# Cross attention in a decoder layer: one exponential over two PSUM banks in place of two, and its place before the copy of the weighed values

## The reference, cut to what matters

```python
q, k, v = query @ Wq, ctx @ Wk, ctx @ Wv          # 32, 8 and 8 heads of 16
q, k = rope(q), rope(k)                           # k and v repeated 4 times
scores = einsum('bhqd,bhkd->bhqk', q, k) / sqrt(16)
probs  = softmax(scores, axis=-1)
ctx    = einsum('bhqk,bhkd->bhqd', probs, v)
x      = x + ctx.reshape(...) @ Wo
```

## Time and profile before

| | us |
|---|---|
| median of 3 runs | 816.56 (815.79 to 816.97) |
| the profiled execution's own time | 816.52 |
| its span in the profile | 814.8 |
| PE busy / DVE / ACT / POOL | 785.9 / 628.3 / 580.2 / 592.5 |
| stretch of the 32 units of cross attention (`x_scores(0)` to `x_weigh(31)`) | 648.3 to 794.8 |

### The profile page before, as it was taken

How to read it: one execution, slowest core, us unless ns; L and a number is a source line. 1 busy time by engine, 2 the same in 40 slices (tenths; PEclk the granted TensorE clock), 3 DMA queues, 4 the chain that set the end, 5 groups by cost and what they waited for, 6 DMA issues and landing times.

```text
span 814.8 us, 17893 instructions
## 1 busy us (share of the span) xinstructions
PE 785.9 (96%) x5641; PEld 388.4 (48%) x5641; DVE 628.3 (77%) x1190; ACT 580.2 (71%) x1070; POOL 592.5 (73%) x537
## 2 busy tenths in 40 slices
PE   4999999999999999999999999999999899999997
PEld 3465444444444444444444444444443445555543
DVE  7767676767767888867778877769887889888876
ACT  7757777777777777777777777778775567556651
POOL 7967999999988888888878888878754755222101
PEclk9999999999999999999999999999999999999999
DMA  9264345533434433344432344443322100000001
GB/s 340 101 206 139 96 138 166 144 121 82 111 97 116 107 82 80 98 96 107 121 92 79 86 97 106 122 146 75 89 54 69 35 3 2 2 15 15 15 27 40
DMA packets 52176, 75.80 MB, mean 93 GB/s; under 512 B 10256, under 2 KB 34096, under 8 KB 51616
## 3 DMA queue, kind: packets, MB, share of 16 engines
q1 hardware_dynamic: 52128, 75.23, 33.1%
HBM read 38.69 MB, written 19.40 MB: 71 GB/s over the span
## 4 chain that ended last, share of the span: by engine, by line
PE 84%; DVE 7%; DMA 3%; SPq 2%; issue 2%; ACT 2%; POOL 0%; DVEq 0%
PE PS L1570 39%; PE PS L1644 7%; PE PS L1611 7%; PE PS L1645 7%; PE PS L1507 6%; PE PS L1659 5%; PE PS L1745 2%; DVE xm L1311 1%; PE PS L1684 1%; PE PS L1621 1%; PE PS L1693 1%; PE PS L1843 1%; DMA KQ<-xmT 1%; PE PS L1809 1%; PE PS L1860 1%
## 5 line engine op out<-in xcount | busy, mean ns | idle before, releaser
L1570 PE MATMUL PS<-XTh,W 128*128 128x512 f16 x1024 | 346.0, 379 | 0.0
L654 POOL TENSOR_TENSOR Pl<-PR,Ph 128x512 f16<-128x512 f32 x254 | 285.8, 1156 | 28.3 <-ACT Ph L936 28.1
L929 ACT ACTIVATE PR<-PS 128x512 f32<-128x512 f32 x256 | 152.8, 597 | 131.4 <-PE PS L1645 124.7
L1125 DVE TENSOR_REDUCE mneg<-PS 128x4 f16<-128x512 f32 x256 | 171.6, 685 | 35.2 <-PE PS L1611 33.5
L1570 PE MATMUL PS<-XTl,W 128*128 128x512 f16 x512 | 193.6, 378 | 0.0
L1113 DVE SCALAR_TENSOR_TENSOR QS<-PS,QC 64x512 f16<-64x512 f32 x256 | 175.5, 685 | 20.3 <-ACT QC L846 16.3
L846 ACT ACTIVATE QC<-PS 64x512 f16<-64x512 f32 x256 | 150.7, 589 | 6.5 <-PE PS L1570 1.6
L1570 PEld LDWEIGHTS PS<-XTh,W 128*128 128x128 f16 x1024 | 96.5, 97 | 119.1 <-issue 25.9
L936 ACT ACTIVATE Ph<-PR 128x512 f16<-128x512 f32 x256 | 139.3, 617 | 0.0
L1611 PEld LDWEIGHTS PS<-KC,QC 112*128 112x128 f16 x1024 | 78.4, 97 | 63.5 <-DVE mneg L1125 2.8
L1611 PE MATMUL PS<-KC,QC 112*128 112x128 f16 x1024 | 99.4, 219 | 0.8 <-ACT QC L846 0.7
(11 more groups left out here) (236 smaller groups left out, 1027.4 us busy)
## 6 DMA issues: line engine op xcount, KB each, us to landing
Wraw<-in_wqr SPq DMA_DIRECT2D x32, 512.0 KB, 4.5
QS<-QC SPq DMA_DIRECT2D x64, 256.0 KB, 3.1
head_outputs<-OS SPq DMA_DIRECT2D x256, 40.0 KB
q_content_parts<-stg SPq DMA_DIRECT2D x12, 256.0 KB, 2.9
k_content_parts<-stg SPq DMA_DIRECT2D x12, 256.0 KB, 3.4
QC<-q_content_parts SPq DMA_DIRECT2D x116, 24.0 KB
KC<-k_content_parts SPq DMA_DIRECT2D x29, 96.0 KB
xs<-in_x SPq DMA_DIRECT2D x8, 256.0 KB, 4.7
```

Source lines behind the costliest of these rows:

```text
L654: nc.gpsimd.tensor_tensor(Pl[:, 4 * j.s + b], PR[:, b], Ph[:, 4 * j.s + b], ALU.subtract).then_inc(s_pl, 1)
L929: nc.scalar.activation(PR[:, b, :], PS[:, bB[b % 2], :], ACT.Exp, scale=ATT_SCALE).then_inc(s_e, 1)
L1125: nc.vector.tensor_reduce(mneg[:, j.p, j.s, :, b], PS[:, bA[b % 2], :].rearrange("p (j k) -> p j k", j=GH), AX.X, ALU.max, negate=True).th ...
L1570: last = mm(PS[:, bQ[c], :], wt[:, j.w, k, c * P:(c + 1) * P], xt[:, k, sl], start=(i == 0), stop=(i == 3 * KT - 1))
```

## The change

The two exponentials of a unit become one instruction that reads banks 4 and 5 as 1024 columns and writes both halves of `XPT`. It waits for both halves of the scores (`2 * u + 2` in place of `2 * u + h + 1`) and adds 2 to `s_ex` at its end. It stands where the exponentials of half 0 stood, so that the whole of it comes before `x_out(u-1)`. In step 8 `norm_high(2, 0)` now comes ahead of it.

```diff
-            def x_exps(u, h):
+            def x_exps(u):
                 if 0 <= u < NU:
-                    act.wait_ge(s_st, 2 * u + h + 1)
+                    act.wait_ge(s_st, 2 * u + 2)
                     if u >= 2:
                         act.wait_ge(s_xo, u - 1)
-                    nc.scalar.activation(XPT[:, u % 2, h], PS[:, 4 + h, :], ACT.Exp).then_inc(s_ex, 1)
+                    nc.scalar.activation(XPT[:, u % 2], PS[:, 4:6, :], ACT.Exp).then_inc(s_ex, 2)
...
                 x_max_out(u + 1)
-                x_exps(u, 0)
                 if u == 8:
                     norm_high(2, 0, bF[0], s_f)
+                x_exps(u)
                 x_out(u - 1)
-                x_exps(u, 1)
```

## The result

The changed kernel takes 818.72 us (median of 7 runs, 818.18 to 820.70), the kernel before 816.86 in the same runs (815.60 to 816.97): a ratio of 1.0032, 95% interval [1.0023, 1.0042]. (The ratio is taken over all runs; the two medians alone give 1.0023.) That is slower, by more than the 0.2% that can be told from no change. The forecast was 817.9 with "the same" as the likeliest outcome. The profiled executions are 818.72 and 816.52, with spans of 817.0 and 814.8; the 2.2 us between them are what has to be found.

A forecast was written before the change was run, and what follows sets the result against it. PE, busy 96% of the span, was taken as the bound, with ACT at 71%. Prices 0.43 + 0.20 + 0.27 + 0.35 + 0.08 gave 1.33 us longer, 817.9 on the median of 816.56; range 816.1 to 819.1.

The forecast's parts named there:

- What the new instruction costs: On ACT, 1024 columns take 1.02 us after a wait, 0.99 back to back; the next instruction starts 0.90 after its start.
- The dearer pair: Rival: the instruction behind the wide exponential starts 1.04 us after it, not 0.90; loss 2.5 us, 819.1; chance 0.23.
- How far the copy moves: `OW` starts 0.43 us later where scores were ready long before, 0.33 where ACT waited, including 0.03 for the fourth matmul.
- Step 2: `x_back` comes straight behind `turn` and waits for `OW`, so PE's list moves by the whole 0.43 us.
- Steps 4 to 6: DMA waits mostly hide the late `x_back` on PE; `rz` and DVE's `O` run late, delaying `outputs_turn`: together 0.20 us.
- Step 27: PE's DMA wait hides `x_back`, but `rz` comes later and DVE's chain to the gate's weights with it: 0.27 us.
- Step 30: No `turn` is left, so `x_back`'s weight load already waits and the next matmul starts later: 0.35 us.
- Behind step 31: `OW` ends 0.33 us later, so the next matmul starts at 794.08 in place of 794.00: 0.08 us.
- Regular r = 3 steps: Steps 6, 10, 14, 18, 22, 26: the next matmul is possible just before it starts now; price 0, no slack left.
- SP's queue and POOL's ... 0: Their releases come from copies ahead of the exponentials or from `query_high`, at most 0.2 us later in step 4; price 0.
- No effect: Rival: PE makes up a late `x_back` at the next DMA wait or in DVE's pace; 816.6 us, chance 0.25.
- faster by `KQ`: Rival: ACT's shorter list lets `KQ` go earlier and PE follows, 3.2 us in all; 813.3 us, chance 0.07.

The follow-up runs named there:

- The order alone: Against the kernel before: still two exponentials of 512 columns, but both ahead of the copy `OW`; 817.63 us, ratio 1.0023.
- The splits: Changed kernel with half, copy, half in units 1, 3, 4, 26, 29, 31: 817.17 us, ratio 1.0012; with 26 useless ACT copies too: 816.83, 1.0007.
- The kernel without the hit: Changed kernel with eight useless one-column copies added to ACT's list behind the sine: 817.70 us, ratio 1.0019 to the kernel before.
- the kernel with one operation behind: Changed kernel with its one exponential of 1024 columns moved behind the copy `OW`; 818.11 us, ratio 1.0026.

## Why the prediction was wrong, by its steps

- **What the new instruction costs: right.** 1.02 and 0.99 us were worked out, 1.02 and 1.00 measured, and 0.90 from start to start in step 2. The dearer pair (1.04) is out. The Trainium skill (ScalarE: Activation LUTs, What ACT_TABLE_LOAD costs) would make it 186 + 0.833 x 1024 = 1039 ns less 93 ns of overlap, 0.95 as an estimate; the trace has 0.90 to 0.92.
- **How far the copy moves: right back to back** (0.43), somewhat short where ACT waits: 0.41 in place of 0.33 behind step 31 (793.04 to 795.48, against a distance of 2.03 in step 31). Waiting for the fourth score matmul adds 0.08 (the exponential starts 0.51 behind the first matmul in place of 0.43), not 0.03.
- **Place by place: the sizes are right within 0.14, the path not in every place.** Step 2: 0.32 for 0.43, since `norm_turn` behind it used to wait 0.39 us for DVE's `pn`, which covered a part. Steps 4 to 6: 0.27 for 0.20, in part by luck. I let a DMA wait cover `x_back` in step 5 and priced DVE's `O` alone; PE's wait for that DMA was only 0.19, so 0.17 were lost in PE's own list before `O` was needed. Step 27: 0.41 for 0.27, the copy being later than I had it. Step 30: 0.34 for 0.35. Behind step 31: 0.15 for 0.08, where 0.06 come from `x_back(29)` in a step that I had at 0. Together 1.49 for 1.33. The order alone reproduces them. The splits take them away in steps 2, 28 and 30, and with the fetch out of the way in steps 4 to 6. Behind step 31 0.15 stay to the end of the span even with the halves split there, so that term isn't shown to be the copy of step 31. Regular r = 3 steps cost 0, as said. The waits went to 15 places and 6.6 us, where about 12 and 4 were expected.
- **"SP's queue and POOL's ... 0" and the regular groups of four "as long as before": here the prediction failed.** The sum had no term for the row maxima's DMA of step 17, 0.64 us. I counted the exponentials as work that ACT is relieved of, and not as places in its list of instructions. The profile of before held what was needed for the warning: packets of kind "instruction" in the page's list of queues, and a DMA on which the scores wait in six places. It could hardly have given the place to within the 0.5 us that decides.
- **The chances.** With the term, 816.52 + 1.49 + 0.64 is 818.65, and 818.72 was profiled; with only the terms that I had, at their true size, it is 818.0, just inside "the same". The kernel without the hit measured 1.0019, which bears that out. The missing 0.64 carried it over the bound. The kernel before was 816.86 beside this result, not 816.56, so the medians differ by 1.86 only: how much of the 0.64 each execution pays is known for the two profiled ones alone (0.64 and 0.60).
- **The rivals.** No effect, and faster by `KQ`: refuted by the stairs, which no later DMA wait makes up, and by `x_rough`'s waits (0.5 us in 2 places, for 0.4 in one). The rule of the Trainium skill (Perfetto Trace Analysis, Optimizing Scalar/DVE Operations) that breaking operations up may let work complete sooner, where an engine isn't saturated but makes others wait, agrees with four of the five terms: with the halves split they are zero (three of them with the split alone, that of steps 4 to 6 with the fetch moved as well).

Open: why 0.33 us of one packet's lateness (726.80 to 727.13) makes the scores 0.9 late when it is the second DMA that is hit, and whether the 0.21 ahead of `xmT` in the kernel with one operation behind are `KQ`'s.

## What to carry to other kernels

Fewer instructions on an engine with slack bring nothing by themselves; look for what the merged operation now stands ahead of, and take a wait of zero cost for a limit just met, not for room to gain. A split has to cover every step with a late copy that is needed at once: the six chosen here left out the step before the last, and 0.15 us stayed behind it. When a change alters how many instructions an engine has, a small DMA on the critical path can fall under that engine's instruction fetch far behind the edit: compare the start of the same matmul in each step, and where one stair stands in unchanged code, move the list by a few idle instructions before believing any other story. Differences of 0.1% between orders of a tuned kernel can be this alone.

## What the runs showed of the hardware that I had not expected

- ACT's instructions come as single packets of 8192 bytes, one for each 124 to 128 of its instructions in the stretch looked at, 0.3 to 0.6 us long; a row-maxima packet that falls behind one is held until it is over (727.13 for 726.80), one of four in each of ten hits. The matmul's wait for the DMA was 0.18, 0.56, 0.57 and 0.85 us in four of them. The 16384-byte packets of queue 8 held none of those of step 17. The Trainium skill (Runtime: NRT & Kernel Launch, Instruction fetch mechanics) says that a list is refilled over a DMA queue of the engine's own in blocks of 16 KiB, 256 instructions, and that it is mostly hidden. By this trace ACT's packets are half that size, and what isn't hidden is their effect on other transfers. The Trainium skill (DMA: Bandwidth & Descriptors, Queues, rings and completion order) says that a DMA engine turns from queue to queue only between packets; the held fourth packet agrees.
- One activation over two banks takes 1.00 to 1.02 us, where two of half the size took 1.05 together: 0.05 us is all that merging saves back to back.
